# Packets, squares, reloads and sums: four joined changes to a graph network kernel

## The chip, the cores and the metric

The kernel runs as one program on one core of a Trainium2 chip. The metric is its device time in microseconds (us). PE is the matrix engine, with its weight loads listed apart as PEld; DVE, ACT and POOL are the vector, scalar and general engines, and SP is the engine that only issues DMAs here. Each runs its own list of instructions in order, and they meet at semaphores.

## What is computed

Four graph blocks work one after the other on 6250 nodes and 106250 edges (`EP` is 106496, 128 x 832, with padding), each on a normalized and rectified `x` and each added to it or put in its place:

```
h = jnp.maximum(_layernorm(x, axis=-1), 0.0)
x = x + _L0_gnn_ref(h, ...)      # attention over the edges, 4 heads
x = x + _L1_gnn_ref(h, ...)      # five convolutions, each with a norm
x = x + _L2_gnn_ref(h, ...)      # the gradient block
x = _L3_gnn_ref(h, ...)          # mean of the neighbours and one matmul
```

One convolution of the second block, and the third block's function, of which the gradient by `xx` is wanted:

```
h = h @ W
h = jax.ops.segment_sum(h[s] * coef, t, num_segments=n) + b
...
def get_H(xx):
    z = xx @ W_fc.T
    e = jax.nn.sigmoid(jnp.concatenate([z[src], z[dst]], axis=-1) @ W_attn.T)
    emax = jax.ops.segment_max(e, dst, num_segments=n)
    w = jnp.exp(e - emax[dst])
    denom = jax.ops.segment_sum(w, dst, num_segments=n)
    h = jax.ops.segment_sum(w / denom[dst] * z[src], dst, num_segments=n)
    h1 = jax.ops.segment_sum((h @ W_encK.T + b_encK)[src], dst, num_segments=n)
    K = _mlp3(h1, K_w0, K_b0, K_w1, K_b1, K_w2, K_b2)
    ue = (h @ W_p1.T + b_p1)[src] + (h @ W_p2.T + b_p2)[dst]
    U = _mlp3(ue, U_w0, U_b0, U_w1, U_b1, U_w2, U_b2)
    E_new = jax.ops.segment_sum(K[src] * U, dst, num_segments=n)
    return jnp.sum(E_new)
```

## The kernel before

**Dense matrices in place of edge sums.** Where a block sums plain node rows over the edges, the kernel has a dense 6250 x 6250 matrix in DRAM: `cells_w` holds the edge weights, `cells_c` and `cells_t` the counts of edges and their transpose. A matrix is read in 50 tiles of 128 x 6250 f32, 3200 KB each, and a 51st tile `HOT`, into three buffers `TILE`; SP issues these reads in `tiles_sp` (L609), and PE multiplies them with the nodes' features (L624). So run the five convolutions `gcn1` to `gcn5` (table "w"; about 4259 to 8510 us of the trace), and later `hsum`, `dh1` and the mean at the end. A row of a tile is 25600 bytes (`NR` is 6400), and `max_dma_last_dim`, 25600 before, is the longest packet in bytes. The matrices are filled by POOL: `put` (L437) writes one value per partition and DMA, 832 of them for a matrix. Those of `cells_c` and `cells_t` run beside `gcn3`, about 5140 to 7450.

**The weighing** ("attend", 8551 to about 9440, and "back", about 13176 to 14020) is the third block's attention. It goes over 200 pieces of 128 x 1600: ACT makes a tanh (L759), an exp (L761) and the square of the tanh (L763), DVE multiplies by the counts (L772) and makes the second weight (L778), PE sums (L787). Of four buffers, the square of the last one is DVE's (L776), as `squared_late` (L749) tells. The counts come in packets of 1600 bytes.

**The edge MLP** `umlp` (26 steps, 10121 to 11650) computes the gradient by U's network and stores two chunks of `d_edges` a step. From 11190 on, POOL scatters these by target into `xd`, so that they lie sorted there: 52 chunks, each loaded into one of three staging buffers (L2117) and put with 16 indirect DMAs (L437). The loop is on L2121: `load(c + 2)`, then a wait for chunk c's load, then the 16 puts. A load waits for all puts of the chunk whose buffer it takes, c−1. Behind chunk 16 POOL does the join and the 50 gathers of the rows at the ends of runs for `umlp`, which are released when `umlp` is done.

**The node chain and `dh1`.** Behind `umlp`, while POOL puts the other 35 chunks, PE and DVE turn and multiply node features (L691 transposes, 400 ahead of the matmuls on L661 and L673; 11732 to 11990), and PE goes through the 51 tiles of `dh1` (`cells_t`; 12004 to 12631).

**The sums by target** ("dsum"): 26 steps over the sorted `xd`, 64 features x 32 edges per partition each. SP loads a step (L2264, `DX`). ACT spreads the masks "same target as the edge before" (L536, L537) and turns the data from edge-major to feature-major (L540) into the single buffer `DM`; DVE adds the carry, scans twice over 32 features and keeps the last column (L553, L558, L560); ACT turns the result back into `DOUT` (L545) and issues its store to `runs` (L547). `prepare_act` begins with a wait for the scan before, since there is one `DM` and one mask in PSUM.

The order on each engine is the order of the code; there is no scheduler.

Of the kernel before, what the change touches and what calls it, by code (L numbers as in the profile page):

```python
# [8 lines left out]
P = 128  # L9
N = 6250  # L10
NT = 50
NR = P * NT
# [4 lines left out]
CJ = 32  # L17
# [58 lines left out]
def build(nc, x_in, src_in, dst_in, src_t_in, w_in, weights_in, vectors_in, out):  # L76
    ctx = ExitStack()
    with ctx:
# [237 lines left out]
        DX = [region(37092 + b * 2048, 2048) for b in range(2)]  # L316
        DM, DOUT = region(41188, 2048), [region(19200, 2048), region(32100, 2048)]
        B33, DHF, GN, YN = region(32100, 33 * NT), region(33750, 1600), region(35428, 33 * NT), region(28850, 33 * NT)
# [285 lines left out]
        def tiles_sp(sp, name, table):  # L604
            for t, (b, n) in enumerate(TAKES[name]):
                if n:
                    sp.wait_ge(S[f"tile_done{b}"], n)
                source = cells(table)[:, t, 0:NR] if t < NT else HOT
                sp.dma_start(TILE[b], source, max_dma_last_dim=4 * NR).then_inc(S[f"tile{b}"], 16)  # L609

# [137 lines left out]

        def squared_late(b):  # L749

            return b == 3

        def weigh_act(act, name, own):
            for k, b, _, phase, t, h in pieces(name, (0, 1)):
                if t == 0 and h == 0:
                    act.wait_ge(S[f"other{phase}"], 16 * (1 + ("attend", "back").index(name)))
                if k >= 4:
                    act.wait_ge(S["weights_used"], k - 3)
                act.activation(groups_of(TANH[b]), piece_of(OTHER[phase], h), ACT.Tanh, bias=own[:, t:t + 1])  # L759
                act.drain()  # L760
                last = act.activation(EXPO[b], TANH[b], ACT.Exp, scale=0.5, bias=half[:])  # L761
                if not squared_late(b):
                    last = act.activation(TANH[b], TANH[b], ACT.Square)  # L763
                last.then_inc(S["weights_made"], 1)

        def weigh_dve(dve, name, phase):
            for k, b, i, _, _, h in pieces(name, (phase,)):
# [5 lines left out]
                if h == 1:  # L773
                    last.then_inc(S[f"part_done{p}"], 1)
                if squared_late(b):
                    dve.tensor_tensor(TANH[b], TANH[b], TANH[b], ALU.mult)  # L776
# [493 lines left out]
        def _(dve):  # L1270
# [394 lines left out]

            begin(dve, carry[:, 0:64], MASK)
            with dve.Fori(0, IT) as it:
                for b in range(2):
                    await_prepared(dve, "dsum", it, b)
                    dve.sem_inc(S[f"free{b}"], 1)  # L1670
                    scan(dve, MASK, DM, 64, carry).then_inc(S["scanned"], 1)
                    dve.drain()
            ends_dve(dve, "dsum", 64)
# [99 lines left out]
        def _(act):  # L1773
# [94 lines left out]
            sums_act(2 * IT - 1)  # L1868
            with act.Fori(0, IT) as it:
                for b in range(2):  # L1870
                    prepare_act(act, "dsum", OD, it, b, (DM, 64), MASK, 32, DX[b])
                    act.wait_ge(S[f"stored{b}"], it * 16 + STORED["dsum"])
                    finish_act(act, "dsum", it, b, 64, R[64], DM, DOUT[b])
            weigh_act(act, "back", a_dst)
# [162 lines left out]
        def _(pool):  # L2037
# [83 lines left out]
            for c in range(52):  # L2121
                if c + 2 < 52:
                    load(c + 2)
                pool.wait_ge(S[f"to_give{c % STAGES}"], 16 * (c // STAGES + 1))
                for j in range(16):
                    put(pool, XD, at_d[:, 16 * c + j:16 * c + j + 1],
                        GS[c % STAGES][:, j * 64:(j + 1) * 64]).then_inc(S[f"given{c % STAGES}"], 16)
                if c == 16:
                    ends_pool(pool, "umlp", OS, P, HD)
# [182 lines left out]
```

## Time and profile before

| | us |
|---|---|
| median of three runs | 14476.57 |
| lowest and highest | 14439.49, 14526.97 |
| profiled execution, own time | 14513.92 |
| its span | 14512.1 |

The profiled execution ran with a mean granted PE clock of 0.635. Its stages, by the times in the trace:

| stage | from, to (us) |
|---|---|
| convolutions 1 and 2 | 4259 to 4655, 4690 to 5061 |
| convolution 3, beside the puts of two matrices | 5097 to 7780 |
| convolutions 4 and 5 | 7790 to 8080, 8100 to 8510 |
| weighing "attend", hsum tiles | 8551 to 9440, 9485 to 9990 |
| edge MLP | 10121 to 11650 |
| puts into `xd` (POOL) | 11190 to 12583 |
| node chain, `dh1` tiles (PE) | 11732 to 11990, 12004 to 12631 |
| sums by target | 12628 to 13003 |
| weighing "back", mean | 13176 to 14020, 14087 to 14475 |

In the rows further down, a line L12 is line 12 of the kernel. Rows of a stretch give the busy time of PE, PEld, DVE, ACT and POOL in this order, each with its count of instructions, then the granted PE clock (PEclk), the mean busy share of the DMA engines and the GB/s. "x26" is a count of instructions. Behind the last bar, or in brackets, stands the idle time of the engine ahead of the instruction and what ended it; "issue" means that it waited for nothing that the profile shows. An instruction's start is in us from the start of the span.

### The profile page before, as it was taken

The numbers are of one execution on the slowest core, as the hardware profiler recorded it, in microseconds if no ns is written. First come the engines' busy times: TensorE is split into PE (matmuls) and PEld (weight loads), VectorE is DVE, ScalarE is ACT, GpSimd is POOL, SyncE is SP. The second block draws the span as 40 slices with busy tenths as digits, with TensorE's granted clock in tenths as the row PEclk, the third lists the DMA queues.
The fourth block names the chain that finished last, engine by engine and source line by source line (L and its number), as shares of the span: only waits on it lengthen the run. The fifth ranks groups of instructions, "written<-read, shape, count | busy, mean of one in ns | idle before, by whom it ended". The sixth has DMA issues, their size and how long they took to land.

```text
span 14512.1 us, 89214 instructions
## 1 busy us (share of the span) xinstructions
PE 5658.6 (39%) x33607; PEld 2598.6 (18%) x33607; DVE 4615.9 (32%) x6087; ACT 2849.1 (20%) x2186; POOL 6329.5 (44%) x6251
## 2 busy tenths in 40 slices
PE   0000000046656732222247557644421424306765
PEld 0000000045542210000012112211421411102221
DVE  4565500034430010000000049900842810027970
ACT  0111000000000000000000039900521600147960
POOL 5555577755540067777740000022876776410000
PEclk5555555555557965555568778966655756658887
DMA  5444220067879931111138875567432536734558
GB/s 192 153 172 162 78 43 21 21 220 286 295 285 405 425 110 40 46 37 46 46 145 367 358 271 185 186 257 280 180 127 87 198 103 232 304 122 161 184 190 382
DMA packets 747819, 2685.46 MB, mean 185 GB/s; under 512 B 195960, under 2 KB 405995, under 8 KB 664792
## 3 DMA queue, kind: packets, MB, share of 16 engines
q1 hardware_dynamic: 517666, 2380.87, 42.7%
q0 software_dynamic: 213744, 171.80, 4.8%
q10 hardware_dynamic: 16070, 128.24, 2.2%
q8 instruction: 216, 3.54, 0.1%
q14 instruction: 123, 1.01, 0.0%
HBM read 1913.69 MB, written 766.75 MB: 185 GB/s over the span
## 4 chain that ended last, share of the span: by engine, by line
another core or an unknown queue 34%; DMA 13%; issue 13%; PE 11%; ACT 10%; DVE 8%; ACTq 4%; POOL 4%; DVEq 2%; SPq 0%; POOLq 0%
DMA arena<-cells_w 8%; PE ps L624 5%; ACT arena L761 4%; ACTq L760 4%; POOL arena L434 3%; ACT arena L759 3%; DMA arena<-cells_c 2%; PE ps L939 2%; DMA arena<-cells_t 1%; DVE arena L558 1%; DVE arena L828 1%; PE ps L918 1%; ACT arena L545 1%; PE ps L912 1%
## 5 line engine op out<-in xcount | busy, mean ns | idle before, releaser
L624 PE MATMUL ps<-arena 128*32 128x400 f32 (+2 forms) x12200 | 2607.9, 713 | 3081.3 <-issue 1471.7
L624 PEld LDWEIGHTS ps<-arena 128*32 128x32 f32 (+1 forms) x12200 | 709.3, 153 | 4975.0 <-issue 3096.5
L787 PE MATMUL ps<-arena 128*33 128x400 f32 x6400 | 1235.0, 534 | 552.8 <-DVE arena L778 551.3
L437 POOL DMA_INDIRECT cells_c<-arena x832 | 843.4, 1014 | 1177.3 <-DVEq L202 879.7
L642 DVE COPY carry<-ps 64x128 f32<-64x128 f32 (+1 forms) x5 | 1.5, 295 | 4047.3 <-PE ps L624 4047.3
L437 POOL DMA_INDIRECT sorted<-arena x832 | 806.9, 970 | 569.9 <-DVE arena L900 299.4
L434 POOL DMA_INDIRECT arena<-t_kv,idx x832 | 802.7, 965 | 568.2 <-DMA idx<-in_src 317.7
L437 POOL DMA_INDIRECT cells_t<-arena x832 | 889.6, 1069 | 275.2 <-issue 275.2
L434 POOL DMA_INDIRECT arena<-t_a,arena x832 | 881.3, 1059 | 278.3 <-issue 278.3
L437 POOL DMA_INDIRECT xd<-arena x832 | 881.0, 1059 | 256.1 <-issue 253.4
L437 POOL DMA_INDIRECT cells_w<-arena x832 | 852.4, 1025 | 287.6 <-issue 287.6
L434 POOL DMA_INDIRECT ends_s<-upto_rows_s,last_s x1 | 1.0, 988 | 2034.8 <-DMA upto_rows_s<-upto_s 2034.8
L1213 ACT ACTIVATE norm_cols<-norm_cols 128x1 f32<-128x1 f32 x5 | 1.0, 203 | 4252.0 <-DVE norm_cols L1195 4252.0
L918 PE MATMUL ps<-arena 128*128 128x150 bf16 (+3 forms) x1456 | 219.4, 292 | 1563.9 <-ACT arena L950 893.9
L772 DVE TENSOR_TENSOR arena<-arena 128x1600 f32<-128x1600 f32 x400 | 727.8, 1819 | 100.2 <-ACT arena L763 66.9
L778 DVE SCALAR_TENSOR_TENSOR arena<-arena 128x1600 f32<-128x1600 f32 x400 | 730.1, 1825 | 33.3 <-issue 2.2
L761 ACT ACTIVATE arena<-arena,half 128x1600 f32<-128x1600 f32 x400 | 651.7, 1629 | 27.8 <-issue 0.3
L787 PEld LDWEIGHTS ps<-arena 128*33 128x33 f32 x6400 | 366.5, 117 | 1418.2 <-DVE arena L778 730.3
L842 PE MATMUL ps<-arena 128*128 128x50 bf16 x832 | 72.4, 219 | 1379.2 <-DVE arena L830 933.2
L558 DVE TENSOR_TENSOR_SCAN arena<-ps,arena 128x512 f32<-128x512 f32 (+2 forms) x494 | 591.2, 1261 | 11.1 <-issue 3.7
L950 ACT COPY arena<-ps 128x200 f32<-128x200 f32 x208 | 67.8, 326 | 2345.4 <-remote 1524.5
L763 ACT ACTIVATE arena<-arena 128x1600 f32<-128x1600 f32 x300 | 456.2, 1521 | 0.0
(515 smaller groups left out, 8712.7 us busy)
## 6 DMA issues: line engine op xcount, KB each, us to landing
arena<-cells_w SPq DMA_DIRECT2D x250, 3200.0 KB, 17.2
arena<-cells_c SPq DMA_DIRECT2D x100, 3200.0 KB, 18.2
cells_w<-arena SPq DMA_DIRECT2D x50, 3200.0 KB
cells_c<-arena SPq DMA_DIRECT2D x50, 3200.0 KB
cells_t<-arena SPq DMA_DIRECT2D x50, 3200.0 KB
arena<-cells_c SPq DMA_DIRECT2D x100, 1600.0 KB, 6.6
arena<-cells_t SPq DMA_DIRECT2D x50, 3200.0 KB
arena<-cells_t SPq DMA_DIRECT2D x100, 1600.0 KB, 6.6
```

What stands on the lines that cost most here:

```text
L434: return pool.indirect_dma_start(dst, None, table, bass.IndirectOffsetOnAxis(ap=index, axis=0))
L437: return pool.indirect_dma_start(table, bass.IndirectOffsetOnAxis(ap=index, axis=0), source, None)
L558: dve.tensor_tensor_scan(to[:, piece], mask[:, 0:n * CJ], buf[:, piece], 0.0, ALU.mult, ALU.add)
L624: mm = pe.matmul(bank[base + k][g * f:(g + 1) * f, 0:m], rows_of, tile[:, g * width + at:g * width + at + m], start=first, stop=last, skip ...
L759: act.activation(groups_of(TANH[b]), piece_of(OTHER[phase], h), ACT.Tanh, bias=own[:, t:t + 1])
L760: act.drain()
L761: last = act.activation(EXPO[b], TANH[b], ACT.Exp, scale=0.5, bias=half[:])
L763: last = act.activation(TANH[b], TANH[b], ACT.Square)
L772: last = dve.tensor_tensor(groups_of(EXPO[b]), groups_of(EXPO[b]), piece_of(PART[p], h), ALU.mult)
L778: dve.scalar_tensor_tensor(TANH[b], TANH[b], -1.0, EXPO[b], ALU.add, ALU.mult).then_inc(S["weighed"], 1)
L787: last = pe.matmul(bank[4 * kind + 2 * h + c][64 * g:64 * g + 33, 0:400], own[:, t, :], moving[:, at:at + 400], start=t == 0, stop=t == NT ...
L918: return pe.matmul(bank[4][:, a * NT:b * NT].rearrange("p (c h) -> p c h", h=NT), hot_lo[k % 2][:, i * P:(i + 1) * P], hot_hi[k % 2][:, i ...
```

## The change

Four edits, in five places.
- `tiles_sp`: for table "w" the last dimension of a DMA is cut at 6400 bytes (NR is 6400; the tables "c" and "t" keep 25600).
- `squared_late` also looks at the name: only in "back" is a square left to DVE. In "attend" ACT makes all 200.
- The sums by target have two mask buffers, two `DM` and the two `firsts`. DVE turns features 0 to 31 of a step (`half_turned`), ACT features 32 to 63 (`before_scan_act`). ACT prepares step k+2 behind the turning back of step k.
- In the loop over 52 chunks, `load(c + 2)` is issued between the eighth and the ninth put of chunk c.

```
@@ tiles_sp
-                sp.dma_start(TILE[b], source, max_dma_last_dim=4 * NR).then_inc(S[f"tile{b}"], 16)
+                sp.dma_start(TILE[b], source, max_dma_last_dim=NR if table == "w" else 4 * NR).then_inc(S[f"tile{b}"], 16)
@@ squared_late, called in weigh_act and weigh_dve
-            return b == 3
+            return name == "back" and b == 3
@@ dsum, DVE
-            begin(dve, carry[:, 0:64], MASK)
-            with dve.Fori(0, IT) as it:
-                for b in range(2):
-                    await_prepared(dve, "dsum", it, b)
-                    dve.sem_inc(S[f"free{b}"], 1)
-                    scan(dve, MASK, DM, 64, carry).then_inc(S["scanned"], 1)
-                    dve.drain()
+            begin(dve, carry[:, 0:64], *DMASK)
+
+            def half_turned(k):
+
+                dve.wait_ge(S[f"loaded{k % 2}"], LOADED["dsum"] + LOADS["dsum"] * (k // 2 + 1))
+                if k >= 2:
+                    dve.wait_ge(S["dsum_out"], k - 1)
+                dve.tensor_copy(by_feature(DM[k % 2], 32), rows(DX[k % 2], 64).rearrange("p j f -> p f j")[:, 0:32, :])
+
+            half_turned(0)
+            for k in range(2 * IT):
+                b = k % 2
+                dve.wait_ge(S["prepared"], PREPARED["dsum"] + k + 1)
+                dve.drain()
+                dve.sem_inc(S[f"free{b}"], 1)
+                scan(dve, DMASK[b], DM[b], 64, carry, goes_on=firsts[b][:]).then_inc(S["scanned"], 1)
+                if k + 1 < 2 * IT:
+                    half_turned(k + 1)
+                dve.drain()
@@ dsum, ACT
-            with act.Fori(0, IT) as it:
-                for b in range(2):
-                    prepare_act(act, "dsum", OD, it, b, (DM, 64), MASK, 32, DX[b])
-                    act.wait_ge(S[f"stored{b}"], it * 16 + STORED["dsum"])
-                    finish_act(act, "dsum", it, b, 64, R[64], DM, DOUT[b])
+
+            def before_scan_act(k):
+                b = k % 2
+                act.wait_ge(S["scanned"], SCANNED["dsum"] + max(1, k))
+                act.copy(by_feature(DMASK[b], 32)[:, :, 1:CJ],
+                         OD.same[:, k * CJ + 1:(k + 1) * CJ].unsqueeze(1).broadcast_to([P, 32, CJ - 1]))
+                act.copy(firsts[b][:], OD.same[:, k * CJ:k * CJ + 1])
+                act.wait_ge(S[f"loaded{b}"], LOADED["dsum"] + LOADS["dsum"] * (k // 2 + 1))
+                act.copy(by_feature(DM[b], 32, 32), rows(DX[b], 64).rearrange("p j f -> p f j")[:, 32:64, :]).then_inc(S["prepared"], 1)
+
+            def after_scan_act(k):
+                b = k % 2
+                act.wait_ge(S["scanned"], SCANNED["dsum"] + k + 2)
+                act.wait_ge(S[f"stored{b}"], STORED["dsum"] + 16 * (k // 2))
+                act.copy(rows(DOUT[b], 64), turned(DM[b], 64)).then_inc(S["dsum_out"], 1)
+                act.drain()
+                act.dma_start(by_edge(R[64])[:, step(k), :], rows(DOUT[b], 64)).then_inc(S[f"stored{b}"], 16)
+
+            before_scan_act(0)
+            before_scan_act(1)
+            for k in range(2 * IT):
+                after_scan_act(k)
+                if k + 2 < 2 * IT:
+                    before_scan_act(k + 2)
@@ xd, POOL
             for c in range(52):
-                if c + 2 < 52:
-                    load(c + 2)
                 pool.wait_ge(S[f"to_give{c % STAGES}"], 16 * (c // STAGES + 1))
                 for j in range(16):
+                    if j == 8 and c + 2 < 52:
+                        load(c + 2)
                     put(pool, XD, at_d[:, 16 * c + j:16 * c + j + 1],
```

POOL around chunk 17, behind the edge MLP, before. `d_edges` is the stored chunk, `given` counts landed puts, `to_give` the landed loads, `ends` gathers read `runs`:

```order
L434 DMA arena<-runs,end_s 128x128 [waits joined]
L434 DMA arena<-runs,end_s 128x128 x49
L2117 DMA arena<-d_edges 128x1024 [waits d_kept1,given1]
L437 DMA xd<-arena 106496x64 [waits to_give2]
L437 DMA xd<-arena 106496x64 x15
L2117 DMA arena<-d_edges 128x1024 [waits d_kept0,given2]
L437 DMA xd<-arena 106496x64 [waits to_give0]
```

and after:

```order
L435 DMA arena<-runs,end_s 128x128 [waits joined]
L435 DMA arena<-runs,end_s 128x128 x49
L438 DMA xd<-arena 106496x64 [waits to_give2]
L438 DMA xd<-arena 106496x64 x7
L2149 DMA arena<-d_edges 128x1024 [waits d_kept1,given1]
L438 DMA xd<-arena 106496x64 x8
L438 DMA xd<-arena 106496x64 [waits to_give0]
L438 DMA xd<-arena 106496x64 x7
L2149 DMA arena<-d_edges 128x1024 [waits d_kept0,given2]
```

The load of `d_edges` stood ahead of all 16 puts of a chunk, and now stands behind eight of them.

ACT in two steps of the sums by target, before; `ps` and `m` are the masks, `loaded` is SP's load, `scanned` is DVE's scan:

```order
L536 ISA [waits scanned]
L536 COPY ps<-same_d 128x32x31
L537 ISA
L537 COPY m<-same_d 128x1
L540 COPY arena<-arena 128x2048 [waits loaded1]
L544 REGISTER_ALU [waits stored1]
L545 COPY arena<-arena 128x2048 [waits scanned]
L547 ISA
L547 DMA runs<-arena 128x2048
```

and after:

```order
L1886 CAST ps<-same_d 128x32x31 [waits scanned]
L1888 CAST first_same<-same_d 128x1
L1890 COPY arena<-arena 128x1024 [waits loaded0]
L1896 COPY arena<-arena 128x2048 [waits stored1,scanned]
L1898 DMA runs<-arena 128x2048
L1886 CAST ps<-same_d 128x32x31 [waits scanned]
L1888 CAST first_same<-same_d 128x1
L1890 COPY arena<-arena 128x1024 [waits loaded1]
L1896 COPY arena<-arena 128x2048 [waits stored0,scanned]
L1898 DMA runs<-arena 128x2048
```

The turn of the data (128x2048 on L540) became half as long, and the masks of a step now stand two steps ahead of its turning back.

ACT in "attend", the third piece, the fourth and the start of the fifth, before:

```order
L759 ACTIVATE arena<-arena,a_src 128x1600
L761 ACTIVATE arena<-arena,half 128x1600
L763 ACTIVATE arena<-arena 128x1600
L759 ACTIVATE arena<-arena,a_src 128x1600
L761 ACTIVATE arena<-arena,half 128x1600
L759 ACTIVATE arena<-arena,a_src 128x1600 [waits weights_used]
```

and after:

```order
L760 ACTIVATE arena<-arena,a_src 128x1600
L762 ACTIVATE arena<-arena,half 128x1600
L764 ACTIVATE arena<-arena 128x1600
L760 ACTIVATE arena<-arena,a_src 128x1600
L762 ACTIVATE arena<-arena,half 128x1600
L764 ACTIVATE arena<-arena 128x1600
L760 ACTIVATE arena<-arena,a_src 128x1600 [waits weights_used]
```

The fourth piece now has its square on ACT as the others do.

## Rows read from the trace of the kernel before

**Rows 1.** The page: the span, the engines' busy time, one row of the DMA issues.
```profile
span 14512.1 us, 89214 instructions
...
PE 5658.6 (39%) x33607; PEld 2598.6 (18%) x33607; DVE 4615.9 (32%) x6087; ACT 2849.1 (20%) x2186; POOL 6329.5 (44%) x6251
...
arena<-cells_w SPq DMA_DIRECT2D x250, 3200.0 KB, 17.2
```

**Rows 2.** Stretches: length, busy us (instructions) by engine, PEclk, DMA share, GB/s.
```profile
4259.00:4655.00 396.00, 222.15 (x1618) 63.55 (x1622) 0.49 (x2) 0.00 (x0) 4.85 (x5) 0.75 1.00 429
8551.00:8980.00 429.00, 303.13 (x1520) 90.25 (x1520) 387.41 (x220) 408.38 (x267) 0.00 (x0) 0.89 0.58 199
8700.00:8850.00 150.00, 112.90 (x554) 33.48 (x552) 141.11 (x80) 147.58 (x97) 0.00 (x0) 0.90 0.57 192
```

**Rows 3.** ACT in order of time (start, length), then DVE's squares in 8551 to 8980.
```profile
8698.92 1.61 ACT L759 ACTIVATE arena<-arena,a_src 128x1600 f32<-128x1600 f32 x1
...
8714.64 1.52 ACT L763 ACTIVATE arena<-arena 128x1600 f32<-128x1600 f32 x1
8716.07 1.62 ACT L759 ACTIVATE arena<-arena,a_src 128x1600 f32<-128x1600 f32 x1
...
L776 DVE TENSOR_TENSOR arena<-arena 128x1600 f32<-128x1600 f32 x24 | 43.6, 1818 | 0.0
```

**Rows 4.** ACT in a sum's step, then groups of ACT and DVE (busy, mean ns).
```profile
12984.97 3.66 ACT L545 COPY arena<-arena 128x2048 f32<-128x2048 f32 x1 [5.34 <-DVE carry L560]
...
12989.27 0.99 ACT L536 CAST ps<-same_d 128x992 f32 x1 [0.65 <-issue]
...
12990.29 3.65 ACT L540 COPY arena<-arena 128x2048 f32<-128x2048 f32 x1
12999.28 3.66 ACT L545 COPY arena<-arena 128x2048 f32<-128x2048 f32 x1 [5.34 <-DVE carry L560]
...
L540 ACT COPY arena<-arena 128x1024 f32<-128x1024 f32 x26 | 50.3, 1934 | 2.3 <-DMA arena<-xq 2.3
...
L1627 DVE COPY arena<-arena 128x2048 f32<-128x2048 f32 x26 | 51.5, 1979 | 3.6
```

**Rows 5.** POOL's waits (total, times, longest), then single instructions of four engines.
```profile
POOL arena L2117 <- DMA xd<-arena: 164.1, 48, 10.5
...
11731.15 0.60 POOL L2117 DMA_DIRECT2D arena<-d_edges  x1
...
11762.72 0.58 POOL L2117 DMA_DIRECT2D arena<-d_edges  x1 [10.51 <-DMA xd<-arena]
...
11760.87 4.35 PE L691 MATMUL ps<-ident,arena 64*64 64x64 f32 x87 [1.14 <-issue]
...
12613.04 0.79 SPq L2264 DMA_DIRECT2D arena<-xd  x2
...
12628.35 3.76 ACT L540 COPY arena<-arena 128x2048 f32<-128x2048 f32 x1 [622.38 <-DMA arena<-xd]
```

**Rows 6.** Stretches, with the columns of rows 2.
```profile
5250.00:5400.00 150.00, 40.78 (x54) 8.25 (x54) 0.00 (x0) 0.00 (x0) 112.25 (x116) 0.52 0.13 44
10690.00:11186.00 496.00, 49.39 (x199) 41.43 (x200) 70.21 (x69) 50.02 (x42) 356.65 (x377) 0.51 0.25 75
11190.00:11650.00 460.00, 208.66 (x1140) 179.28 (x1140) 395.35 (x389) 291.61 (x226) 330.35 (x275) 0.70 0.51 192
11740.00:11752.00 12.00, 1.05 (x4) 0.89 (x5) 0.00 (x0) 0.00 (x0) 9.26 (x10) 0.50 1.02 281
11763.00:11783.00 20.00, 9.09 (x113) 6.21 (x110) 3.43 (x4) 0.00 (x0) 15.12 (x17) 0.67 0.18 53
12450.00:12600.00 150.00, 66.27 (x368) 16.24 (x362) 0.00 (x0) 0.00 (x0) 86.56 (x91) 0.67 0.72 285
14087.00:14475.00 388.00, 218.71 (x1599) 62.16 (x1600) 1.56 (x3) 0.00 (x0) 0.00 (x0) 0.75 0.99 423
```

**Rows 7.** PE's second matmul of the node chain, 11881 to 11990.
```profile
L673 PE MATMUL ps<-folded,arena 64*64 64x32 f32 x200 | 22.0, 285 | 37.6 <-issue 32.8 <-DVE arena L1659 4.8
```

More of the change, by code:

```diff
@@ L316, in build @@
         DX = [region(37092 + b * 2048, 2048) for b in range(2)]
-        DM, DOUT = region(41188, 2048), [region(19200, 2048), region(32100, 2048)]
+        DM, DOUT = [region(41188, 2048), region(34148, 2048)], [region(19200, 2048), region(32100, 2048)]
+        DMASK = [ps[:, b * 1024:b * 1024 + 32 * CJ] for b in range(2)]
         B33, DHF, GN, YN = region(32100, 33 * NT), region(33750, 1600), region(35428, 33 * NT), region(28850, 33 * NT)
@@ L747, in pieces, with squared_late @@
                 yield base + k, k % 4, k // 2, k // (2 * NT), k // 2 % NT, k % 2
-        def squared_late(b):
-            return b == 3
+        def squared_late(name, b):
+            return name == "back" and b == 3
         def weigh_act(act, name, own):
@@ L761, in weigh_act @@
                 last = act.activation(EXPO[b], TANH[b], ACT.Exp, scale=0.5, bias=half[:])
-                if not squared_late(b):
+                if not squared_late(name, b):
                     last = act.activation(TANH[b], TANH[b], ACT.Square)
@@ L774, in weigh_dve @@
                     last.then_inc(S[f"part_done{p}"], 1)
-                if squared_late(b):
+                if squared_late(name, b):
                     dve.tensor_tensor(TANH[b], TANH[b], TANH[b], ALU.mult)
```

## The prediction

> **What bounds the kernel now.** I read the page first, for the span and the busy shares, then cut the span into stages with the table of stretches, and asked in each which engine the others wait for. No engine bounds the whole: PE is busy for 39% of 14512.1 us, POOL 44%, DVE 32%, ACT 20% [rows 1]. The stages follow one another, so each part of the change is priced in its own. The profiled execution's own time is 14513.92 us, 37.4 above the median of 14476.57. The sum starts from the profiled time, and 37.4 comes off at the end.
>
> **Part A, packets of 6400 bytes for the convolutions.** It touches 255 transfers of 3200 KB (250 tiles of `cells_w` [rows 1], 5 of `HOT`). The layers without puts beside them stand on these: in the first, the DMA engines are busy for 1.00 of the stretch at 429 GB/s [rows 2]. No row shows a packet of 6400 bytes. One bound is the attention stage, whose matrices come in packets of 1600 bytes: a share of 0.58 for 199 GB/s is 343 GB/s for a full share, against 429, so a byte costs up to 25% more there [rows 2]. A cost that goes with the number of packets grows by 15 units between 25600 and 1600 bytes and by 3 of them between 25600 and 6400, so 25% becomes 5%. All 255 tiles, 3.28 MB each at 429 GB/s, are 1948 us, of which 5% is 97. The other bound is nothing. In the attention stage gaps and other transfers count in the share too, and in layer 3 some tiles hide beside a slow PE, so I stay nearer to the low end: **+25 us**, range 0 to +97.
> The Trainium skill, page "DMA: Bandwidth & Descriptors", section "Why small descriptors are slow", speaks against this edit: each packet pays about three bus cycles on top of one for every 32 bytes. An estimate from that page is 203 cycles four times against 803, 1.1% of 1948, so 21 us where the sum has 25. At 1600 bytes it would give 6%, and the row has 25; the trace doesn't settle which.
>
> **Part B, forward squares on ScalarE.** The weighing works on 200 pieces of 128x1600, and of each four DVE squares one. In 8700 to 8850 ACT is busy for 147.58 of 150 us, DVE for 141.11, PE for 112.90 [rows 2]; a group of four pieces takes 17.15 us on ACT (8698.92 to 8716.07) [rows 3]. ACT sets the pace, and the edit gives it more. A square holds it for 1.43 us from its start to the next instruction's (8714.64 to 8716.07), or 1.52 by its own duration [rows 3]. The 50 moved ones cost 50 x 1.43 = **+71 us** (76 by the duration). DVE is relieved of 50 instructions of 1818 ns [rows 3], but behind a busy ACT that only becomes waiting. Nothing hides the cost.
>
> **Part D, sums by target over two steps.** Before, each of the 26 steps is a serial chain across ACT and DVE: from one turning back to the next, 12984.97 to 12999.28, is 14.31 us, of which ACT waits 5.34 for DVE [rows 4]; 26 of them are 372. After, ACT does for each step the turning back with the store's issue (4.30 until the masks, 12984.97 to 12989.27), the masks (1.02 until the turn of the data, 12990.29), and half of that turn. The half is 128x1024, for which a row of another stage has 1.93 us [rows 4]. Sum 7.25, plus 0.3 for two semaphores: 7.55 us. DVE does its scan and what stands with it, the 5.34 that ACT waits now, and the other half of the turn, 1.0 by the 1.98 of a DVE copy twice as long [rows 4]. That is 6.3, less than 7.55: ACT bounds the stage and hides the scan. A fill of 8.2 (half turn, masks, first scan), 26 x 7.55 = 196, less 3.0 since the last step prepares nothing: 201 us. **−171 us.** Bounds: with a half turn as dear as a whole one (3.66) a step is 9.3 and the gain 126; with no semaphore time it is 179. Load and store of a step, 2.1 MB, then flow at 278 GB/s, and 429 is seen [rows 2].
>
> **Part C, the reload amid the puts.** Before, POOL issues the load of chunk c+2 ahead of the puts of chunk c, and the load waits until those of chunk c−1, issued just before, have landed: 164.1 us in 48 waits, the longest 10.5 [rows 5]. After, it stands behind eight more puts (10 us), so the wait goes. For the 35 chunks behind the edge MLP that frees 35/48 x 164 = 120 us of POOL. But POOL is no end by itself: PE runs the node chain (L691, L661, L673) and the tiles of `dh1` beside it, and SP issues the sums' loads behind the last of those tiles (12613.04); the first sum starts at 12628.35 [rows 5]. Behind the moved load on POOL's queue stand only the other eight puts; SP's queue has nothing of this.
> What does PE do while POOL issues without a break? Beside the unbroken puts of layer 3 it runs 54 matmuls and 54 weight loads in 150 us, one instruction in 1.39, with a DMA share of 0.13. From 10690 to 11186, beside unbroken gathers, it is 199 and 200 in 496, one in 1.24. In the node chain it is 9 in 12 us [rows 6]. Then POOL waits 10.51 us for its puts, and towards the end of that wait PE runs 87 matmuls in 4.35 us (11760.87) [rows 5]. After it, with a short wait in each chunk, PE does 113 and 110 in 20 us [rows 6]. So **the waits that part C takes away are what lets PE through.** Why, no row tells; I take it as the trace shows it.
> The price if PE stays at 1.40: POOL comes to the puts behind the edge MLP at 11731 as now [rows 5] and needs 35 x (16 x 1.29 + 0.9) = 754 us, with 150/116 = 1.29 from layer 3 [rows 6]. It ends at 12485. By then PE has done some 752/1.40 = 537 of the 800 instructions (400 pairs) of L691. Then all is fast: 7 us for the rest, 90 for L661 and L673 (109 now, of which L673 alone waits 32.8 for "issue" [rows 7]), and a gap of 14 as now: 12596. Of 51 tiles three are loaded by then; 48 at 388/50 = 7.76 us, the pace of the last stage [rows 6], are 372. The sums start at 12968, not at 12628. **+340 us**, range +250 (some bursts remain) to +440 (puts at 1.40, tiles beside other transfers).
>
> **Sum, case S:** 14513.9 + 25 + 71 − 171 + 340 = 14779, less 37.4: **14742 us**. Its own range is 14620 to 14880.
>
> **Rivals.**
> G, PE goes its own way: the stream of puts isn't what slows it. Then part C is a gain. The puts end 118 us earlier, and the last stretch of `dh1`, 368 matmuls (11.5 tiles) in 150 us at 285 GB/s [rows 6], so 13.0 a tile, goes at 7.76 for 11 tiles: −55. 14513.9 + 25 + 71 − 171 − 55 = 14384, less 37.4: **14347 us, faster.** For it: the edge MLP runs at 2.48 matmuls per us from 11190 to 11650 beside puts [rows 6], though with a wait in every chunk; and cause and effect could stand the other way round, since a PE that draws tiles fills the DMA engines and makes puts land late. It decides at one point, whether PE's rate in the 750 us behind the edge MLP follows the breaks in POOL's row.
> The Trainium skill, page "SBUF — State Buffer", section "SBUF: two separate sides", gives this rival's result: PE has its own ports and never waits on another engine, only DVE and GpSimd block each other. The slow rows in three places speak against this being the whole story.
> M, PE is slowed but gets through: the load in the middle of each chunk, or a full queue, breaks POOL's row now and then, and part C costs 130 us, somewhat over a third of S's. 14569 − 37.4 = **14532 us.**
> S+, the edge MLP stays slow too: it got fast at 11190, when POOL had to wait for its first chunk. If that isn't enough, it goes on at 199/496 = 0.40 matmuls per us, not 2.48 [rows 6], until POOL has put chunk 16 and waits for it, 17 x 21.5 = 366 us later: 366 x (1 − 0.40/2.48) = 307 more, **15049 us.** Against it: the first chunk still has to land ahead of the first put.
> Part C not doing what it says: if the waits only move into the middle of the chunk, it costs nothing, and the sum is 14439 − 37 = 14402. I count it with G; eight puts are 10 us, about the longest wait that there is now.
>
> **How the numbers follow.** S 0.50, G 0.22, M 0.15, S+ 0.13. S leads because the same slow step stands in three stages with an unbroken POOL, and the burst of 87 inside a POOL wait. Predicted is the time of S, 14742. The range reaches from G to the upper end of S, 14320 to 14880, and leaves out S+ and tails, under 0.2. Half a percent (72 us) is about what a measurement of this kernel can tell from no change. Faster by more is below 14404: G, 0.21. Within it: most of M, 0.10. Slower: S, S+ and the rest of M, 0.69.
>
> **What would show it.** Part A: in the first two layers the same DMA share with fewer GB/s, 400 to 429. Part B: a group of four pieces at 18.58 us, ACT busy all the time. Part D: turnings back 7.5 us apart, no long wait of ACT for DVE. Part C: POOL's waits ahead of the load gone, its last put some 100 us earlier, PE in steps of 1.40 through the node chain until then, and the tiles of `dh1` behind the last put. The prediction is wrong if PE does several instructions per us in the node chain while POOL goes unbroken (G), if the edge MLP loses 300 us (S+), or if a step in D isn't near 7.5.

## The result: slower by 1.6% in the measured pair

| us | before | after |
|---|---|---|
| median of six runs | 14483.94 | 14926.93 |
| lowest and highest | 14439.49, 14802.54 | 14688.89, 15229.49 |
| profiled execution, own time | 14513.92 | 14821.94 |

The ratio is 1.0156 with a 95% interval of 1.0108 to 1.0204, and leaves out runs more than 1.5% above the fastest of their kernel. That is some 14710, where 14742 was forecast; the median of all six lies above the forecast range, since half of the runs of after took 15032 to 15229.

For the comparison of stages I use first and last starts of reads and puts, which any part of the change leaves in place. All in us, profiled executions:

| stretch | before | after | difference | forecast |
|---|---|---|---|---|
| first to last read of `cells_w` | 4234 | 4273 | +39 | +25 |
| from there to the first read of "attend" | 66 | 69 | +3 | 0 |
| "attend", first to last read | 858 | 921 | +63 | +71 |
| edge MLP, first load to last store | 1519 | 1588 | +69 | 0 |
| from there to the sums' first load | 983 | 1318 | +335 | +340 |
| sums' first load to the first read of "back" | 533 | 339 | −193 | −171 |
| all others | 6319 | 6312 | −7 | 0 |

The sum is 308 before rounding, the difference of the two spans.

The node chain is where the time went. These are single instructions of after, first POOL's last two puts, then PE's transposes (start, length, idle time before).

```profile
12671.52 0.97 POOL L438 DMA_INDIRECT xd<-arena  x1 [0.43 <-issue]
12672.92 0.97 POOL L438 DMA_INDIRECT xd<-arena  x1 [0.43 <-issue]
```
```profile
12668.49 0.26 PE L692 MATMUL ps<-ident,arena 64*64 64x64 f32 x1 [2.54 <-issue]
12671.29 0.26 PE L692 MATMUL ps<-ident,arena 64*64 64x64 f32 x1 [2.54 <-issue]
...
12678.29 0.26 PE L692 MATMUL ps<-ident,arena 64*64 64x64 f32 x1 [1.14 <-issue]
12679.00 4.09 PE L692 MATMUL ps<-ident,arena 64*64 64x64 f32 x70 [0.44 <-issue]
```

PE issues a transpose every 2.80 us, with its weight load between two, for as long as POOL puts and for 6 us more, and then runs the last 70 in 4.09 us. POOL's puts come 1.40 us apart here too. Over the whole stretch (11887 to 12673) only half of them do, and the others come 1.27 to 1.30 apart, while PE keeps to its 1.40. The four stretches below (columns as in rows 2) show the same from afar: the first layer, the slow stretch of the edge MLP, a part of the node chain, and `dh1`.

```profile
4259.00:4655.00 396.00, 226.54 (x1614) 63.17 (x1606) 0.49 (x2) 0.00 (x0) 0.00 (x0) 0.75 1.02 418
10650.00:11276.00 626.00, 75.61 (x307) 62.88 (x305) 105.36 (x103) 76.47 (x62) 453.99 (x477) 0.51 0.26 79
11900.00:12330.00 430.00, 40.38 (x155) 27.25 (x155) 5.59 (x5) 0.00 (x0) 306.18 (x324) 0.50 0.20 58
12690.00:13110.00 420.00, 239.19 (x1768) 75.96 (x1764) 16.49 (x26) 1.11 (x2) 0.00 (x0) 0.72 0.92 371
```

The 155 transposes and 155 loads in 430 us are one instruction in 1.39 us, the pace of convolution 3 in [rows 6]. `dh1` then runs at 371 GB/s with nothing beside it. The first layer draws 418 GB/s where it had 429 [rows 2], its DMA engines fully busy in both.

POOL's waits in the stretch of the puts, the counterpart of the first line of [rows 5] (total, times, longest):

```profile
POOL xd L438 <- issue: 305.9, 831, 1.1
POOL joined L435 <- DVEq L580: 111.0, 1, 111.0
...
POOL arena L2149 <- issue: 1.2, 3, 0.8
```

The 164.1 us of waiting for landed puts are gone. In their place POOL waits 111 us, once, for the edge MLP, and what it saved has bought nothing.

ACT in "attend", two starts four pieces apart, and one step of the sums on ACT and then DVE, against [rows 3] and [rows 4]:

```profile
8759.05 1.61 ACT L760 ACTIVATE arena<-arena,a_src 128x1600 f32<-128x1600 f32 x1
...
8777.62 1.61 ACT L760 ACTIVATE arena<-arena,a_src 128x1600 f32<-128x1600 f32 x1
```
```profile
13290.11 3.69 ACT L1896 COPY arena<-arena 128x2048 f32<-128x2048 f32 x1
13293.87 0.33 ACTq L1898 DMA_DIRECT2D runs<-arena  x1
13294.24 0.99 ACT L1886 CAST ps<-same_d 128x992 f32<-128x992 bf16 x1 [0.43 <-issue]
...
13295.25 1.93 ACT L1890 COPY arena<-arena 128x1024 f32<-128x1024 f32 x1
13297.09 3.71 ACT L1896 COPY arena<-arena 128x2048 f32<-128x2048 f32 x1
```
```profile
13295.45 1.03 DVE L1674 COPY arena<-arena 128x1024 f32<-128x1024 f32 x1
13297.34 0.35 DVE L554 SCALAR_TENSOR_TENSOR arena<-carry,first_same,arena 128x64 f32<-128x64 f32 x1 [0.85 <-ACT arena L1890]
```

The four pieces take 18.57 us (18.58 forecast). A step of the sums takes 6.98 us (13290.11 to 13297.09), ACT turns back without waiting for DVE, and DVE waits for ACT.

### The profile page after: what moved, and what is told of

Its sections match the earlier page's. It is cut to its first block, busy times and chain, and to the rows that moved or that the text cites. A ratio compares the mean times of both kernels' runs of the same rounds, so it can differ in the third digit from the quotient of the medians.

```text
span 14820.1 us, 89042 instructions
## 1 busy us (share of the span) xinstructions
PE 5587.6 (38%) x33607; PEld 2592.3 (17%) x33607; DVE 4567.0 (31%) x6064; ACT 2876.3 (19%) x2236; POOL 6334.8 (43%) x6251
## 4 chain that ended last, share of the span: by engine, by line
another core or an unknown queue 31%; issue 16%; DMA 14%; PE 12%; ACT 10%; DVE 8%; ACTq 5%; POOL 3%; DVEq 2%; SPq 0%; POOLq 0%
DMA arena<-cells_w 8%; PE ps L625 5%; ACT arena L762 4%; ACTq L761 4%; ACT arena L760 4%; POOL arena L435 2%; DMA arena<-cells_c 2%; DMA arena<-cells_t 2%; PE ps L940 2%; DVE arena L559 1%; ACT arena L1834 1%; DVE arena L829 1%; PE ps L919 1%; PE ps L913 1%
## 5 line engine op out<-in xcount | busy, mean ns | idle before, releaser
L625 PE MATMUL ps<-arena 128*32 128x400 f32 (+2 forms) x12200 | 2570.3, 717 | 2943.9 <-issue 1250.4
L788 PE MATMUL ps<-arena 128*33 128x400 f32 x6400 | 1191.8, 518 | 658.7 <-DVE arena L779 658.1
L764 ACT ACTIVATE arena<-arena 128x1600 f32<-128x1600 f32 x350 | 532.1, 1520 | 0.0
```

Source lines behind the costliest of these rows:

```text
L625: mm = pe.matmul(bank[base + k][g * f:(g + 1) * f, 0:m], rows_of, tile[:, g * width + at:g * width + at + m], start=first, stop=last, skip ...
L788: last = pe.matmul(bank[4 * kind + 2 * h + c][64 * g:64 * g + 33, 0:400], own[:, t, :], moving[:, at:at + 400], start=t == 0, stop=t == NT ...
```

## The experiments

The same three lengths are taken from every run: the transposes of the node chain, from the first one to the first read of `dh1`, which SP issues when the 400 are done, the whole from the edge MLP's last store to the sums' first load, and the edge MLP itself. "Waits" are POOL's waits for landed puts of `xd`.

| kernel | waits | transposes | last store to sums' load | edge MLP | sums | "attend" |
|---|---|---|---|---|---|---|
| before | once a chunk | 170 | 983 | 1519 | 533 | 858 |
| after | none | 795 | 1318 | 1588 | 339 | 921 |
| e1, reload only | none | 795 | 1321 | 1718 | 533 | 858 |
| e2, all but reload | once a chunk | 154 | 960 | 1840 | 333 | 920 |
| e3, after and a wait | once a chunk | 145 | 1281 | 1192 | 332 | 921 |
| e4, before and waits in the matrix puts | once a chunk | 201 | 966 | 1847 | 524 | 858 |
| e12, after without squares | none | 795 | 1325 | 1468 | 339 | 858 |
| e10, sums only | once a chunk | 24 | 1288 | 1187 | 327 | 849 |
| e9, reload only | a few | 21 | 1200 | 1185 | 518 | 849 |
| e11, reload and sums | a few | 22 | 1186 | 1182 | 328 | 849 |
| e8, after again | a few | 22 | 1175 | 1192 | 328 | 920 |

The last four rows belong to runs in which PE wasn't held beside POOL at all; they come further down.

**The reload alone (e1).** On the kernel before:

```
             for c in range(52):
-                if c + 2 < 52:
-                    load(c + 2)
                 pool.wait_ge(S[f"to_give{c % STAGES}"], 16 * (c // STAGES + 1))
                 for j in range(16):
+                    if j == 8 and c + 2 < 52:
+                        load(c + 2)
```

> Only the load amid the puts, on the kernel before. Theory (an unbroken row of DMA issues on POOL holds PE at one instruction in 1.40 us): PE stays slow through the node chain until POOL's last put, the sums by target start some 335 us later than before counted from the last store of the edge MLP, and the time is 14484 + 335 = 14819, or 60 to 70 more where the slow stretch of the edge MLP also lasts longer. Rival (the slow node chain of the changed kernel comes from the other parts, by packets or by the later stages' timing): within 60 us of before, or 55 less.

Measured: 15070.24 (14769.11 to 15129.85), the kernel before 14502.79 beside it (13 runs, 14450.70 to 14725.92). The transposes take 795 us as in after, so the reload does it by itself. The median is 250 above the forecast. The profile (span 15021.9) says why: against before's, the node chain and `dh1` have 338 us more and the edge MLP 199, which the reload doesn't touch.

**All but the reload (e2).** The changed kernel with the loop over chunks as before.

> The changed kernel without the moved load: packets of 6400 bytes, forward squares on ScalarE, pipelined sums. Theory: +39 for the layers, +63 for the squares, -193 for the sums as in the two traces, so 14484 - 91 = 14393, a ratio of 0.994, and PE gets through the node chain in 150 us as before. Rival (the sums or packets bring the slow chain): 14710 as the whole change.

Measured: 14710.47, ratio 1.0123 (1.0056 to 1.0189). The time was not forecast: I wanted 14393 and the rival had 14710. But the transposes took 154 us, so the rival's reason is wrong as well. Packets, squares and sums are as in after, 4267, 920 and 333 us. What the sum lacked is the edge MLP: it took 1840 us, 321 more than before. No part of the change touches it.

```profile
10200.00:11100.00 900.00, 103.10 (x444) 85.99 (x444) 158.18 (x153) 106.30 (x91) 656.92 (x688) 0.53 0.26 78
```

This is its slow stretch: 444 matmuls in 900 us beside 688 POOL instructions, where [rows 6] has 1140 in 460. So the hold that the reload brings on in the node chain comes and goes in the edge MLP, not at all in e3, for 500 us or for 1000 in others, and it is the largest part of the difference between the profiles of these kernels: 1192 to 1847 us over seven profiles with the same code there.

**The whole change and one wait (e3).** The load stays amid the puts; ahead of the 16 puts:

```
+                if c >= 1:
+                    pool.wait_ge(S[f"given{(c - 1) % STAGES}"], 256 * ((c - 1) // STAGES + 1))
```

> The whole change, and one more wait: ahead of the 16 puts of a chunk POOL waits until the puts of the chunk before have landed. The load stays amid the puts. If the break in POOL's row is what lets PE through, the node chain is fast again and the time is that of the change without part C, near 14400. If it is where the load stands (its own descriptors between the puts), nothing is won: 14710 plus 35 to 50 for the waits.

Measured: 14459.14 (14367.68 to 14740.61, 10 runs), ratio 0.9948 (0.9908 to 0.9987). The first read of `dh1`, POOL's new wait, and the transposes:

```profile
L610 SPq DMA_DIRECT2D arena<-cells_t x50: 319/319/432, 11913.6 to 12410.1; - x50
```
```profile
POOL xd L438 <- DMA xd<-arena: 209.2, 49, 15.0
```
```profile
11768.00:11914.00 146.00, 45.02 (x402) 31.37 (x404) 14.36 (x15) 0.00 (x0) 96.85 (x103) 0.51 0.31 100
```

402 matmuls in 146 us, and the reading of `dh1` begins at 11913.6. In after the same work took 795. The only difference in the code is a wait of POOL, 209.2 us in 49 times, so the break in POOL's row is what lets PE through; where the load stands does not matter. One rival is chance, since PE isn't held everywhere in this profile: in the edge MLP it goes freely beside gathers, and POOL waits for nothing between them.

```profile
10200.00:11180.00 980.00, 420.64 (x2122) 361.82 (x2122) 740.70 (x726) 533.93 (x427) 779.53 (x700) 0.66 0.51 180
```

The steps between PE's instructions speak against chance in the node chain. In 22 places there e3 has the step of 1.40 us (1.38 to 1.42), as before has in 29, e2 in 32 and e4 in 32, and e9, where PE wasn't held, in none; after, e1 and e12 have it in 476 to 479. So PE was held in e3's chain too, and let through again and again. All four profiles with a wait in each chunk have 145 to 201 us for the transposes, all three without 795.

This run's last store to sums' load is still 1281 us, since its edge MLP was done at 11386, early, and POOL had its first 17 chunks to put ahead of the gathers on which the node chain waits; the sums' first load comes 2 us behind POOL's last put. The total is a little better than before's, by less than the sums gave.

**Without the squares (e12).** The whole change with `squared_late` as before.

> The whole change without the forward squares on ScalarE. Where PE isn't slowed beside POOL's row (before: 10976, whole change: 10596), the attention stage is 849 to 858 us again and not 920: 10596 - 65 = 10531, a ratio of 0.959, the best of all versions. Where it is slowed: 14710 - 63 = 14647, a ratio of 1.011, still slower than before. Rival: ACT's extra squares hid something, and the gain is under 20.

Measured: 14833.12 (14650.77 to 14989.46, 4 runs), the kernel before beside it 14764.45 (14413.97 to 14930.42, 7 runs). With runs 500 us apart no ratio can be given. The stages still tell: "attend" 858 us, the squares' 63 taken back, and the transposes 795 us, for the third time to the same microsecond.

**Matrix puts in sixteens (e4).** The kernel before; in the loops over `cells_c` and `cells_t`:

```
+                if c % 16 == 15:
+                    pool.wait_ge(S["cells_c"], 16 * (c + 1))
```

> The kernel before, with a wait for all puts so far after each 16 of the 1664 puts of cells_c and cells_t, beside convolution 3. 104 waits of 1.48 us lengthen POOL's row from 2310 to about 2460 us. If a wait lets PE through anywhere, PE does about 66 instead of 14 instructions in 20 us as in the node chain, convolution 3 is done in some 900 us instead of 2680, convolutions 4 and 5 follow under the puts as well, and the bound is POOL's row (5140 + 2460 = 7600) ahead of the attention stage at 8551: up to 950 us less, 13500 to 13900. If the waits help only where DMA lands into few queues or only L691, PE stays at 1.40 and the time is 14484 + 150 = 14630.

Measured: 14338.19 (14272.80 to 14769.00, 5 runs), ratio 0.9850 (0.9767 to 0.9933). The layers took 3977 us instead of 4234, a quarter of the hoped-for gain.

```profile
5137.00:5400.00 263.00, 190.91 (x812) 63.20 (x808) 2.51 (x3) 0.00 (x0) 152.96 (x158) 0.86 0.87 346
6200.00:7400.00 1200.00, 330.77 (x427) 66.99 (x426) 0.00 (x0) 0.00 (x0) 830.70 (x859) 0.51 0.12 41
```

In the first 263 us PE did 812 matmuls beside 158 POOL instructions. Without the breaks, in the six other profiles in which PE was held, it was down to some 18 matmuls in 50 us within 110 us of the first put. Between 5400 and 6000 it goes up and down (12 to 175 in 50 us), and from 6200 on it did 427 in 1200 us, one instruction in 1.41, with a break of POOL every 16 puts. So these breaks keep PE free for a while and release it now and then, but from 6200 on they don't. Beside a free PE, its reads fill the DMA engines (0.87), and POOL's breaks are longer, 58.1 us in 10 waits; from 6200 on they are 100 us in 53, 1.9 each. That this loop is why either condition lasts is my reading. No run sets the length of the breaks by itself. The total says less than the layers do: with the edge MLP 328 us longer in this profile than in before's, 257 us less in the layers would not show.

**Three kernels that met no held PE.** Next I tried to lengthen POOL's breaks. e5 stores each chunk of gathers right behind its 16 gathers (`keep(c)` for `keep(c - 1)`). e6 lets POOL wait, after each 16 matrix puts, for three more tiles of layers 3 to 5:

```
+            turns = TAKES["gcn3"] + TAKES["gcn4"] + TAKES["gcn5"]
+            def in_turn(k):
+                if 3 * k < len(turns):
+                    b, n = turns[3 * k]
+                    pool.wait_ge(S[f"tile_done{b}"], n + 1)
...
+                if c % 16 == 15:
+                    in_turn(c // 16 + 1)
```

e7 cuts the tiles of table "w" into packets of 1600 bytes (`NR // 4`).

> The kernel before; POOL stores each chunk of gathered a2 rows right behind its own 16 gathers, so that it waits for them to land once a chunk, where before it stored the chunk before and hardly waited. Theory (a pause of POOL lets PE through): the edge MLP has no slow stretch of 500 to 600 us and takes 1100 to 1300 us from its first load to its last store, not 1519, although 52 waits of about 1.5 us lengthen POOL's gathers by 80; the time falls by 200 to 400, to about 14200. If pauses of 1.5 us are too short once the slow state has set in (as they were behind 6200 us in the run with matrix puts in sixteens), the stretch stays and the time is 14500 to 14580.

> The kernel before; after each 16 puts of cells_c and cells_t POOL waits until PE has done three more tiles of convolutions 3 to 5 (153 tiles against 104 groups). Theory (PE's slow state is held by POOL's unbroken issues and left in any long enough pause, whatever POOL waits for): the three layers run beside the first half of the puts at about 10 tiles in 100 us, convolution 5 ends near 6700 and the puts near 7800, and the attention stage begins near 7850 instead of 8559: 14484 - 650 = about 13830, with the lottery of the edge MLP's slow stretch on top. If the slow state isn't left in these pauses, three tiles take 230 us between groups of 16 puts, and the time grows by thousands. If what counts is that POOL's own DMAs drain, the result lies between.

> The kernel before with packets of 1600 bytes for the convolution tiles. From the first tile's issue to the last one's the layers take 4218 to 4234 us with 25600 bytes and 4257 to 4273 with 6400, 39 us more. If the price goes with the number of packets it is five times that, +195, and layer 1 shows about 380 GB/s at a full share. By the attention stage's row (25% a byte) it would be +450 and 343 GB/s. The time, apart from the edge MLP's stretch: 14680 or 14930.

Measured: e5 11065.92, ratio 1.0082 (1.0063 to 1.0102); e6 10988.49, ratio 1.0009 (0.9995 to 1.0023); e7 10940.50 in one run; and the kernel before, beside them, **10983.09** (13 runs, 10957.97 to 11003.58). The same kernel takes 3500 us less than in the runs before, on the chip with the same number (12) as e1 to e4. Of this, 1671 us lie ahead of the first tile and 1972 in the layers (before's profile against e10's). Here is a stretch in which both kernels have the same code:

```profile
1705.00:2400.00 695.00, 42.80 (x262) 37.25 (x262) 69.36 (x150) 4.80 (x13) 519.09 (x516) 0.50 0.19 32
```
```profile
1705.00:2400.00 695.00, 623.20 (x4317) 554.22 (x4317) 483.55 (x1077) 50.05 (x154) 502.29 (x519) 0.50 0.96 350
```

POOL has 516 and 519 instructions in these 695 us, at the same pace. PE has 262 matmuls in one and 4317 in the other. The granted clock is 0.50, its lower level of 1.2 GHz, in both, so what holds PE isn't the clock. Nor is it in the code, or in the chip alone, by its number. The hold was there in the pair that was forecast and in e1 to e4 and e12 (chip 11), and absent in e5 to e7 and e8 to e11 (chip 3).

One number tells the two conditions apart: how often two successive starts of PE's instructions, weight loads included, lie 1.395 to 1.405 us apart. In before it is 1234 times, in the other profiles of the held kind 921 (e4) to 1610 times (e1), and in e5 to e11 once or never. POOL has this step too where PE is held, between its indirect DMAs: 305 to 1418 times, against one to three. Where PE has other engines to wait for, the same rate shows as bursts: in before's stretch above it does 56 instructions in 3.81 us and then none for 74.59, five times over, which is 78.40 us or 56 times 1.40.

That leaves e5 and e6 without an answer to their question. What e5 does show is the price of its breaks where there is nothing to gain, 120.4 us of waits and 0.8%. In e7 the layers take 2433 us, against 2262 with 25600 bytes in e10 of the next set: +171 where 195 was forecast by the number of packets. The rate goes with that number, roughly: in 2700 to 3400, with the DMA engines at a full share, it is 412 GB/s in e10, 404 with 6400 bytes (e8), 2% less, and 367 in e7, 11% less for five times as many more packets. The time of the whole kernel doesn't: e7's one run is 43 us shorter than the kernel before, for a reason that comes with the next set.

**The change and its parts where PE is free (e8 to e11).** e8 is the changed kernel, e9 the reload alone, e10 the sums alone, e11 both.

> The whole change, once more, beside runs of the kernel before on the same chip. Beside the last three kernels the kernel before took 10983 us, with no slow PE anywhere beside POOL's row: 4312 matmuls in 1705 to 2400, where the first profile has 262. If it is so here too, POOL's row of puts bounds the stage behind the edge MLP (1359 us from the first put of xd to the last), and the moved load is a gain of 130 to 200: -165 there, +45 for the packets, +63 for the squares, -190 for the sums, 10983 - 247 = about 10740, a ratio of 0.977. If PE is slow beside POOL as in the first profile: 14710, a ratio of 1.016. If the forecast's ground (the waits let PE through) is wrong in itself, the change is slower or the same in both.

> Only the load amid the puts. Where PE isn't slowed by POOL's row: a gain of 130 to 200, 10983 - 165 = 10818. Where it is: 14820 to 15070 as in its first run.

> Only the sums by target over two steps. They don't stand beside POOL, so -190 to -200 whether PE is slow beside POOL or not: 10983 - 190 = 10793, or 14484 - 195 = 14289.

> The two parts that gain where PE isn't slowed, without packets and squares: 10983 - 165 - 190 = 10628, the best of all. Where PE is slowed: 14484 + 335 - 195 = 14624, and the sums alone are better.

| kernel | median | ratio to before (10975.85, 7 runs) |
|---|---|---|
| e8, whole change | 10596.41 | 0.9658 (0.9641 to 0.9675) |
| e9, reload | 10859.17 | 0.9899 (0.9881 to 0.9917) |
| e10, sums | 10783.92 | 0.9834 (0.9815 to 0.9853) |
| e11, both | 10686.79 | 0.9745 (0.9727 to 0.9762) |

The same change that was 1.6% slower is 3.4% faster here. 10740 was forecast for it, and 10628, as the best of all, for e11. The sums give 192, the 190 forecast. The reload gives 117, less than 165: POOL's waits for landed puts are not all gone, by e10's and e8's rows.

```profile
POOL arena L2149 <- DMA xd<-arena: 184.6, 48, 12.8
```
```profile
POOL arena L2149 <- DMA xd<-arena: 65.7, 16, 10.4
```

Where `dh1`'s reads fill the DMA engines the puts take more than eight puts' time to land, and 16 waits stay.

The surprise is that the whole change beats e11 by 90 us, though it adds 71 us of squares (920 against 849). Part A must give some 160 us. The stages show 119 of them ahead of "attend" and 21 between the first read of `hsum` and the edge MLP's first load; no run tells why it is these 21. The 119 come so: POOL puts the sorted edges beside the first layers here, and waits for them to land.

```profile
L438 POOL DMA_INDIRECT sorted<-arena x832: 963/969/4025, 2550.3 to 3827.3; - x167
```
```profile
L438 POOL DMA_INDIRECT sorted<-arena x832: 966/972/3852, 2553.2 to 3657.9; - x167
```
```profile
2700.00:3400.00 700.00, 487.24 (x2852) 162.81 (x2846) 16.33 (x43) 3.26 (x2) 397.15 (x407) 0.84 0.98 412
```
```profile
2700.00:3400.00 700.00, 476.85 (x2816) 159.78 (x2810) 16.34 (x43) 3.25 (x2) 512.85 (x526) 0.85 0.99 404
```

With packets of 25600 bytes the 832 puts take 1277 us (2550.3 to 3827.3), with 6400 bytes 1105 (2553.2 to 3657.9). In 2700 to 3400 POOL gets 526 instructions through, not 407 (one in 1.33 us, not in 1.72), while the tiles lose 2% (404 against 412 GB/s). The matrices' puts then start at 3728 and not at 3908, and "attend", which waits for them, begins 68 us behind the last tile instead of 188. The Trainium skill, page "DMA: Bandwidth & Descriptors", section "Queues, rings and completion order", says that a DMA engine goes round its queues packet by packet. The page's packet is a group of descriptors, and no row shows how long such a turn is. If a turn holds as many pieces of the tiles in both kernels, a put waits for a quarter of the bytes here, and the shorter puts agree with that. e7, with 1600 bytes, has the 832 puts take 1106 us and those of the matrices start at 3730, no earlier than with 6400 bytes: at one put in 1.33 us POOL is near the 1.27 at which it puts with nothing in the way.

No version was found that is best in both cases. Where PE is free it is the whole change (10596); without the squares it would be about 70 less by the stage lengths, but e12, the run of that version, met the other case. Where PE is held, the sums with POOL's waits kept are the best part by the stages (333 us for 533 in e2; the sums alone were not run there), and e4's breaks had the lowest median (14338), within the scatter of the edge MLP.

## Why the prediction was right, point by point, and where it wasn't

**The case.** S was forecast, by name: no break in POOL's row, PE at 1.40 us an instruction until the last put. It is shown by e1 (reload alone, 795 us), e2 (all else, 154) and e3 (reload with a wait, 145). The burst of 87 matmuls inside a wait in [rows 5] was the row that said so.

**Part C, +340, measured +335.** The size is right partly by luck, since its terms were off on both sides. The puts behind the edge MLP took 785 us (11887.56 to 12672.92) where I had 754: half of them come 1.40 us apart and the mean is 1.36, not 1.29. PE had done 327 and 328 of the 400 pairs when they ended (537 of 800 instructions forecast), so the rest was as short as forecast, some 10 us. L661 and L673 then took 33 us for my 90, which I had read from rows where PE was half held, and the gap of 14 was 0. The tiles took 414 (12717.04 to 13131), for 372. And `dh1` has 50 tiles and two buffers; I wrote 51, of which three loaded. The step held, PE done behind the last put.

**Part D, −171, measured −193.** A step takes 6.98 us, not 7.55. The 0.3 us for semaphores don't exist, since DVE's scan is done before ACT looks for it; from the turning back to the masks is 4.13 us, not 4.30, and from the half turn to the turning back 1.84, not 1.93.

**Part B, +71, measured +63** (62 in e2, 71 where PE is free).

**Part A, +25, measured +39** in the layers where PE is held, and nothing there where PE is free (2266 against 2262 us), with a gain by the sorted puts, 172 us shorter, that the forecast didn't have. I named every queue that the reload moved past, and not the puts that stand beside the tiles. In the profile of before those end at 4264, six us behind the first tile's read, so no row of it could show this.

**S+**, the edge MLP slow for longer, is true in small: the slow stretch went from 496 us to 626 (+69 in the stage). It isn't the change that does it. Profiles with the same code there have 1192 to 1847 us, so it could as well have been −327 or +328. The range had no term for that, and half of the runs of after lie above it.

**G**, faster, had 0.22 with PE not slowed by POOL's row. That is just what e8 found in another set of runs, 0.9658. Its time was not G's 14347, because all stages beside POOL were shorter. Its gain was not G's either, 380 us for 130: by the runs where PE is free, part A gave some 160 where G's sum has +25, and part C 117 where it has 55. The Trainium skill's page "SBUF — State Buffer", section "SBUF: two separate sides", says that PE never waits for another engine at its ports. PE's rate in e5 to e11 fits that; in the others its rate follows POOL's breaks, and no run shows whether a port has to do with it. The forecast treated as a property of the kernel what is one of the runs. That the whole hold could be absent, the rows of before couldn't tell. But they had one stretch that the forecast left out, the beginning of the edge MLP:

```profile
10200.00:10600.00 400.00, 184.18 (x946) 158.04 (x944) 328.51 (x323) 247.34 (x191) 321.08 (x276) 0.67 0.52 187
```

PE does 946 matmuls in 400 us beside 276 instructions of POOL, which waits for nothing that the profile shows. The same code has 199 in 496 us from 10690 on. POOL's instructions last 1.16 us each here and 0.95 there [rows 6]; whether that lets PE through or comes of a free PE, no run shows. In any case a row of POOL without a wait doesn't always hold PE, not even in this profile. That the node chain would be held was right in all three profiles without waits, but the rows didn't make it certain.

## What to carry to other kernels

An engine's wait that looks like pure loss can be the break in which another one works; before removing it, look at what the others do inside it and right behind it. Where PE goes at a constant step per instruction (1.40 us here), waiting for "issue", next to an unbroken row of POOL's DMAs, count what it does in POOL's breaks, and look for the same step in other runs of the same kernel. Measure such a change in more than one set of runs, and compare stage by stage: "back" took 856 to 858 us in every profile, and the transposes 795 in three, where the totals scattered by 3%.

## What the runs showed of the hardware

- PE beside an unbroken row of indirect DMAs on POOL: one instruction in 1.40 us in some sets of runs, and no slowing in others (262 against 4317 matmuls in 695 us), with the same code and the same granted clock. The step of 1.40 us stands 921 to 1610 times in each profile of the one kind and at most once in one of the other. Even in the first kind PE is free in some stretches in which POOL waits for nothing (946 matmuls in 400 us in before, 2122 in 980 in e3). The node chain's 400 pairs took 21 to 24 us where PE was free; where it was held, 145 to 201 with POOL's breaks, and 795 without. What differs between the sets, and why PE is held at all, stays open: no kernel could set it.
- With a break of POOL every 16 puts PE was free at first (e4: 812 matmuls in 263 us, breaks of 5.8 us) and held later (427 in 1200, breaks of 1.9 us). Which of the two, the breaks or the free PE, brings the other, no run shows.
- Packets of 6400 bytes instead of 25600 on a queue at full share cost it 2% (412 to 404 GB/s), and let another queue's puts through 29% faster (407 to 526 POOL instructions in 700 us).
